# Which engine issues the DMA of a head group's negated maxima in a four-unit attention kernel: SyncE's queue or ScalarE's

## What is computed

```python
x = x + tanh(g_xattn[0]) * cross_attention_0(ctx, layernorm(x), b, seq_len)   # unit 0
x = x + tanh(g_ffn[0])   * attention_plus_experts(layernorm(x))               # unit 1
x = x + tanh(g_xattn[1]) * attention_over(x, ctx)(layernorm(x))               # unit 2
x = x + tanh(g_ffn[1])   * causal_attention_then_top2_experts(layernorm(x))   # unit 3
```

## Time and profile before

| | |
|---|---|
| median of 3 runs | 3029.32 us (3022.75 to 3034.18) |
| the profiled execution: its time, its span | 3026.3 us, 3024.5 us |
| TensorE busy | 2484.4 us, 82% |
| VectorE busy | 1736.7 us, 57% |
| ScalarE busy | 1165.0 us, 39% |
| GpSimd busy | 752.9 us, 25% |
| mean granted TensorE clock | 0.897 |

### The profile page before, as it was taken

The page is one execution under the profiler, slowest core; times in us unless marked ns, Lnnn a source line. Parts: engine busy times, 40 slices in busy tenths (PEclk is TensorE's granted clock), DMA queues, the critical chain, the costliest instruction groups (busy, mean ns, idle before and its releaser), DMA issues. The chain is left out here.

```text
span 3024.5 us, 51264 instructions
## 1 busy us (share of the span) xinstructions
PE 2484.4 (82%) x17380; PEld 1619.6 (54%) x17381; DVE 1736.7 (57%) x4456; ACT 1165.0 (39%) x2426; POOL 752.9 (25%) x1410
## 2 busy tenths in 40 slices
PE   2677799899999778899889889999545999999930
PEld 1333455455555444555555567777344767676720
DVE  7566688677777556566666646665446222222238
ACT  1444563233433325565556554555320111111111
POOL 4233331211222131222212222333000222222221
PEclk8777899899899889999899999999855999999975
DMA  8677754443534365665556664666272100100034
GB/s 234 146 159 141 170 102 87 78 73 67 87 63 81 55 117 88 112 109 99 91 97 113 113 109 86 124 127 121 83 271 81 32 31 32 34 31 32 31 124 167
DMA packets 338613, 302.13 MB, mean 100 GB/s; under 512 B 20133, under 2 KB 298447, under 8 KB 338160
## 3 DMA queue, kind: packets, MB, share of 16 engines
q1 hardware_dynamic: 316240, 255.33, 42.0%
q10 hardware_dynamic: 15264, 26.22, 2.5%
q0 software_dynamic: 6912, 17.97, 1.9%
HBM read 205.57 MB, written 93.22 MB: 99 GB/s over the span
## 5 line engine op out<-in xcount | busy, mean ns | idle before, releaser
L1066 DVE TENSOR_REDUCE mx<-s_ps 128x2 f32<-128x512 f32 (+2 forms) x1280 | 796.0, 658 | 408.0 <-PE s_ps L834 189.3
L959 ACT ACTIVATE ex<-t_ps 128x512 f32<-128x512 f32 (+1 forms) x1280 | 684.6, 576 | 427.4 <-PE t_ps L870 393.8
L870 PE MATMUL t_ps<-qs,ks 102*128 102x256 bf16 x2048 | 392.0, 294 | 127.6 <-DMA qs<-mt 109.0
L892 PE MATMUL pv_ps<-ex,va 128*32 128x256 f32 (+1 forms) x5120 | 340.8, 396 | 3.9 <-ACT ex L959 3.5
L870 PEld LDWEIGHTS t_ps<-qs,ks 102*128 102x128 bf16 x2048 | 176.8, 103 | 280.0 <-DMA qs<-mt 118.0
L810 PE MATMUL pre_ps<-wexp,xt 128*128 128x512 f32 x512 | 248.5, 618 | 15.1 <-DVE moe L1134 14.8
L1584 PE MATMUL x_up_ps<-wup,x_rows_t 128*128 x568 | 257.9, 597 | 1.9 <-issue 1.3
L1603 PE MATMUL x_y_ps<-wdn,x_act 128*128 x1136 | 257.0, 379 | 0.9 <-ACT x_act L1630 0.9
L1650 DVE TENSOR_TENSOR x_pre<-x_up_ps,bup 128x512 f32<-128x512 f32 x142 | 98.3, 692 | 233.0 <-PE x_up_ps L1584 233.0
L1000 POOL TENSOR_SCALAR mp<-mx 128x16 bf16<-128x16 f32 x128 | 34.5, 269 | 783.0 <-DVE mx L1066 780.0
L842 PE MATMUL s_ps<-ks,qs 99*128 99x256 bf16 (+1 forms) x1024 | 198.5, 297 | 33.4 <-DVE mx L1066 21.2
(11 more groups left out here) (264 smaller groups left out, 3910.1 us busy)
## 6 DMA issues: line engine op xcount, KB each, us to landing
q_parts<-pq SPq DMA_DIRECT2D x64, 384.0 KB, 6.3
qs<-q_parts SPq DMA_DIRECT2D x64, 384.0 KB, 5.2
qs<-q_parts SPq DMA_DIRECT2D x192, 128.0 KB, 6.0
k_parts<-pk SPq DMA_DIRECT2D x48, 384.0 KB, 2.9
ks<-k_parts SPq DMA_DIRECT2D x48, 384.0 KB
ks<-k_parts SPq DMA_DIRECT2D x144, 128.0 KB
ks<-ctx_k_parts SPq DMA_DIRECT2D x32, 384.0 KB
ks<-ctx_k_parts SPq DMA_DIRECT2D x96, 128.0 KB
```

Source lines behind the costliest of these rows:

```text
L870: last = pe.matmul(dst[:, t * T:(t + 1) * T], key[0:ROWS, h, t * P:(t + 1) * P], qs[q_at][0:ROWS, h, :], start=True, stop=True)
L892: last = pe.matmul(pv_ps[i * VW:(i + 1) * VW, q0:T], val[:, t, k * QH + i, :], e, start=r == 0 and t == 0, stop=r == srcs - 1 and t == NT - 1,
L959: act.activation(ex[:, n % EXPS, 0:w], t_ps[n % 2][:, 0:w], ACT.Exp).then_inc(t_read, 1)
L1066: dve.tensor_reduce(dst, s_ps[n % 2][:, 0:w].rearrange("p (a b) -> p a b", a=parts), AX.X, ALU.max).then_inc(s_read, 1)
```

## The change

MT loses its SP stage and its wire; a new step MOVE, behind MT, has them on ScalarE. The wait on `tr_read` (set by the copy L954) and the DMA go to ScalarE's loop. MOVE gets the same rank as MT.

```diff
-    "S": [("pe", 0.28), ("dve", 0.69)], "M": [("pool", 1.3)], "MT": [("pe", 0.2), ("act", 0.4), ("sp", 0.5), ("wire", 2.3)],
+    "S": [("pe", 0.28), ("dve", 0.69)], "M": [("pool", 1.3)], "MT": [("pe", 0.2), ("act", 0.4)], "MOVE": [("act", 0.75), ("wire", 2.3)],
...
-        m = add("MT", g, add("M", g, *ss))
+        m = add("MOVE", g, add("MT", g, add("M", g, *ss)))
...
-    return 0 if op[0][0] in ("OT", "FIN", "M", "MT") else 1
+    return 0 if op[0][0] in ("OT", "FIN", "M", "MT", "MOVE") else 1
...
 @block.sync
-                    elif name == "MT":
-                        sp.wait_ge(tr_read, TR_AT[step] + 1)
-                        sp.dma_start(qs[q_at][BIAS:ROWS, k * HG:(k + 1) * HG, :], mt[(2 * j + k) % 4][:, :]).then_inc(max_rows[q_at][k], 16)
...
 @block.scalar
                     elif name == "MT":
                         act.wait_ge(tr_ready, TR_AT[step] + 1)
                         act.activation(mt[(2 * j + k) % 4][:, :], tr_b[0:3 * HG, 0:T], ACT.Copy).then_inc(tr_read, 1)
+                    elif name == "MOVE":
+                        act.wait_ge(tr_read, TR_AT[("MT", u, b, k)] + 1)
+                        act.dma_start(qs[q_at][BIAS:ROWS, k * HG:(k + 1) * HG, :], mt[(2 * j + k) % 4][:, :]).then_inc(max_rows[q_at][k], 16)
```

## The result

The median went from 3026.03 us (3020.97 to 3034.18, 4 runs) to **3053.35 us** (3039.12 to 3056.81, 4 runs). The ratio is 1.0078, with a 95% interval of 1.0054 to 1.0103: slower, by more than the 0.5% that the prediction took as the limit of what can be told. The prediction said 2969, with a range up to 3040. It was wrong in sign and in size. The profiled execution of the changed kernel took 3039.1 us, 14 us under its median.

A forecast was written before the change was run, and what follows sets the result against it. TensorE, busy 82% of the span, was taken as the busiest engine, its largest idle cause late DMAs of the maxima. Terms -95 - 20 + 40 + 15 = -60 us gave 2969 us, own range 2930 to 3005, wider range 2905 to 3040.

The forecast's parts named there:

- The move leaves SyncE's list: SyncE saves 128 issues, 93 us, and 415 us of standing for ScalarE's copy; nothing counted for what it issues next.
- The move leaves SyncE's queue: Landing of the maxima takes 1.8 us on ScalarE's queue; TensorE's 119.2 us of waits shrink by 95, bounds 45 and 119.
- the undisturbed row: Profile row of a move with nothing large ahead: T begins 1.3 us after the issue's end, the landing's lower bound.
- the 95 us taken off: TensorE's waits for the maxima saved: 44 us in unit 0, 27 in unit 1, 17 in unit 2, 7 in unit 3.
- The clock: Of 328 us at the low clock level in units 0 to 3, at most 164 could come back; 20 us taken off.
- Units of work change places: In unit 2 the first S stands earlier, so its wait for the context's rows grows: +40 us, bounds 15 and 127.
- Unit 3 keeps its length: Listed among the signs that the forecast is right: unit 3's time does not change.
- ScalarE issues: 128 issues put 93 us more on ScalarE's list, mostly hidden; +15 us for delayed exponentials, bounds 0 and 93.
- The landing does not get shorter: Rival, 8%: the move's packets still queue behind bulk, only SyncE's lateness of 45 us goes; 3039 us.
- Unit 2's loads become the bound: Rival, 12%: a store ahead of LOADV lengthens unit 2's wait at the first S, about 127 us instead of 40; 3056 us.
- The issue queue: Rival, 17%: ScalarE's issue can't begin during a long one of SyncE, mostly in unit 2, 45 us more; 3014 us.

The follow-up runs named there:

- e1: Kernel before with its old lists, but ScalarE instead of SyncE issues each move right behind its copy: 3004.42 us, ratio 0.9951.
- e4: Probe without computation, a 12 KB move from SyncE, ScalarE or GpSimd, alone or behind bulk; ScalarE's landed after 0.9 and 1.4 us alone, 5.3 to 8.6 behind bulk.
- e3: Changed kernel's order, but GpSimd issues each move, put into its list by planned time: 3090.27 us, ratio 1.0239.
- e5: Changed kernel, but the planner counts 8.0 us instead of 2.3 for a move's landing in unit 2: 3024.35 us, ratio 1.0006.
- e10: Changed kernel, but unit 2 alone is planned with the costs of before, ScalarE still issuing every move: 3002.56 us, ratio 0.9918.
- e8: Kernel before, SyncE issuing the moves, plus a spare 12 KB DMA issued by ScalarE behind each of 128 copies: 3026.99 us, ratio 1.0007.

## Why the prediction was wrong

By its own steps:

- **The move leaves SyncE's list: right.** SyncE's 415 us of standing for the copy are gone, and ScalarE's issues take 728 to 1380 ns with a median of 729. I counted nothing for what SyncE issues next; e1 shows no gain beyond the moves' own waits. The share of the waits that is SyncE's lateness I gave as 38% from two cases whose sums don't give it exactly; e1 measures 39 of 119 us, 33%.
- **The move leaves SyncE's queue: this step failed.** I took 1.8 us for the landing, near the undisturbed row, on the reckoning that the packets of two queues alternate. They don't here while earlier loads are under way: 1910 packets of q1 passed before the first of q10. Behind bulk the landing is 4.4 to 9.2 us from any issuer (e4) and 7.7 in the median for unit 2's late moves, around the row that I had as the upper bound. The row of 1.3 us showed that bulk ahead is what costs, and I read it as bulk ahead *in the same queue*. Of the 95 us taken off, the waits gave back 20 in unit 0 and 31 in unit 1, where 44 and 27 stood, and added 57 in unit 2 and 8 in unit 3. In unit 0 other loads became late next, as forecast: the wait for the context's load went from 1.4 to 16.7 us. The rule of the Trainium skill that I leaned on, "DMA: Bandwidth & Descriptors", "Queues, rings and completion order", that the engines take turns between queues packet by packet, does not describe the 6.7 us before the move's first packet; the 1.3 us after it agree with it, 27 packets of q10 beside 441 of q1. The one that I weighed against it, in "Issuing engines are not separate DMA queues" of the same page, agrees with e1, e3 and e4: only the sequencer's time is saved. I gave that rival 8%.
- **The clock: nearly the right sum, in the wrong places.** The time at the low level went from 156 to 120 us in unit 0, from 82 to 24 in unit 1, from 82 to 133 in unit 2 and from 7 to 17 in unit 3. By the two levels that gives back 16 us, where I took off 20, but unit 0's part is within its scatter. The granted clock rose from 0.94 to 0.98 in unit 1 and fell to 0.91 in unit 2. By the two levels that is 29 of the 57 us gained in unit 1, the waits for moves being the other 31, and about 26 of the 51 lost in unit 2. In these two units the clock doubled the change, of either sign.
- **Units of work change places: the right unit and nearly the right size, but the wrong wait.** I said +40 us in unit 2, at the first S. It was +51, at the first T. I had looked for what the new order does to the loads and not for what it does to the move, whose cover I had just declared sufficient. The S came early enough to wait, but TensorE reached it late, held by T. That the term was real all the same shows in e5, where it stands at 76.8 us as soon as T no longer holds TensorE.
- **Unit 3 keeps its length: wrong, 27 us.** I had read the new lists at three places, none in unit 3. e10 shows that they cost 23 us.
- **ScalarE issues, +15: too much.** e8 gives 0 to within 0.3%. ScalarE stood 394 us for TensorE's T already.
- **The rivals.** "The landing does not get shorter" named the mechanism, and its 3039 was the profiled execution to a fraction of a microsecond; that is luck, since it knew nothing of unit 3 and of the 31 us in unit 1. "Unit 2's loads become the bound" had the sign and the place but not the wait; its 3056 is 3 us from the median, and that is luck too, since the wait that it counted on fell to 0.4 us. The issue queue did not show: 14 of ScalarE's moves begin in the midst of an issue of SyncE of over 1 us, as the row at 1427.43 does, and 13 of them take 0.73 to 0.76 us. The one of 1.38 us is ScalarE's first, and e4's first took 1.31 with nothing beside it.

What stays open: how unit 2's 51 us split between the shorter cover of the moves and their later landing, since no list was tried that changes only one of the two. The medians allow an estimate: copy, issue and landing now take 0.4 + 0.7 + 7.7 = 8.8 us against 3.3 us of cover. With the old landing of 4.8 and the new cover some 2.6 us a job would be left, with the new landing and the old cover of 7.0 some 1.8, so neither alone explains it. Open too is what the small waits come from that make up most of unit 3's loss.

## What to carry to other kernels

Here, moving a small DMA to another engine's queue saved what its old engine was late with, and no more. Where bulk is in flight, count the landing as the trace shows it behind bulk, and ask at which moment of the bulk it will be issued. Before a difference of some us in one stage is called a gain, look at the other traces in which that stage is the same; here such traces lay 12 us apart. Where a planner or scheduler rebuilds the lists, test the new order and the new mechanism apart, and stage by stage; here the first cost 3.25% and the second gave 0.5 to 2.4%. And combine the stages that gained: that gave 1.6%, from a change that as a whole lost 0.8%.

## What the runs showed of the hardware that I had not expected

- A DMA of 12 KB waited 6.7 us for its first packet while 1910 packets of another queue passed, and then took under 1.3 us. In e4 it landed after 0.9 to 1.4 us alone, after 7.0 to 9.2 behind loads in pieces of 512 B, and after 4.4 to 5.6 behind loads in rows of 4 KB, for SyncE, ScalarE and GpSimd alike. Its first packet began when about as many packets had begun as were handed over ahead of it (2097 to 2434 against 2304, and 384 to 420 against 384).
- 128 more DMA issues on an engine that is 39% busy (e8) cost between -0.14% and +0.27%.
